# Moving the masks of one attention quad and four value products, with other PSUM banks, in a two-layer transformer block kernel

## The chip, the cores and the metric

The kernel runs on one core of one Trainium2 chip. The metric is the time of one execution on the device, in microseconds (us); the figure that counts is the median of several runs.

## The reference, cut to what matters

Input `x` has 16 batches of 256 tokens with 128 features, all float32.

```python
xn = layernorm(x)
x  = x + favor(xn) + local(xn)       # first block
xn = layernorm(x)
x  = x + attention(xn) + experts(xn) # second block

# favor (causal linear attention, 16 heads of 8, 32 random features)
phi_q, phi_k = exp(x_h @ proj.T - 0.5 * sum(x_h ** 2)) / sqrt(32)
num[t] = sum_{s <= t} (phi_q[t] . phi_k[s]) v[s];  den[t] = sum_{s <= t} phi_q[t] . phi_k[s]
favor  = layernorm(num / den @ out_w + out_b + x)

# local: 2 layers, each
h = shift_token(x); q, k, v = split(h @ wqkv)      # 8 heads of 64
q, k = rotary(l2norm(q) * q_scale), rotary(l2norm(k) * k_scale)
x = x + softmax(window(q @ k.T)) @ v @ wo          # window of 64 + 64
x = x + (a * gelu(g)) @ w2 + b2                    # a, g = layernorm(shift_token(x)) @ w1 + b1

# attention: 16 heads of 8, softmax over 256 keys
# experts: 8 experts of 256, the best two of each token weighted, and a shared one
```

## The kernel before, in words

The 16 batches are done two at a time, in 8 turns. In a turn T = 512 tokens lie on the free axis. All instructions are written out by hand, per engine, in one list each (`@block.tensor`, `@block.scalar`, `@block.vector`, `@block.gpsimd`, `@block.sync`), and ordered across engines by counting semaphores alone: `now(name, n)` is the count that a semaphore has after the n-th event of this turn.

PSUM has 8 banks. Every product that an engine will read back is a **job** `(name, k)` with a bank. The function `job` (called in the order in which PE will do the jobs) gives each a bank from a ring (`RINGS`, `RING_OF`), and notes who used the bank last and what frees it: `pe.wait_ge(*freed(name, k))` ahead of a job makes PE wait until the former user's reader is done. So the ring decides for whom a product has to wait.

A turn is, in this order: **layer 0** of the local block, **layer 1** of it, then the second block (router, experts with the attention's maxima between them, attention). The favor attention is spread through the two layers, in 8 **quads** of 4 heads (`FAVOR_AT`, `FAVOR_PV`): `favor_score` (L635, L639 on PE, into 4 banks), the causal mask as a multiply on DVE (L1472, frees each bank with `favor_p`), `favor_pv` (L652, accumulates numerator and denominator of half the batches in one bank for 4 quads), and after the fourth quad a copy to `heads` on ACT (L1220), `favor_den` (L659, spreads the denominators over rows) and on DVE `favor_out` (reciprocal L1462 and multiply L1463).

One layer, in the names of the code:

- `loc_raw` (L712): queries and keys, 8 products; DVE rotates them (L1492 to L1501, tile `lc`), ACT squares them, PE sums the squares (L698, L732).
- DVE turns the sums into roots (`rsqrt`, L1343 to L1350, and three bf16 parts up to L1517, semaphore `loc_rs`); PE transposes them (L742), ACT copies them to `lrT` (L1216), and PE spreads them over the rows: 4 products `loc_rb` (L751). DVE multiplies `lc` with them, 8 multiplies (L1525), each counted by `loc_qk`.
- **Maxima**: in two groups g = 0 and 1, PE first writes the window mask into 4 banks (L758, "claims" the banks), then adds 96 short products (L770, `loc_max`); group g reads the `lc` of the first (g = 0) or last (g = 1) four multiplies. DVE reduces the four banks (L1531, `loc_mx`) and writes negated maxima (`loc_nm`).
- PE transposes these (L782) and, for each of 4 units k, writes the scores (`loc_sT`: L794, L802, L810), ACT takes the exponentials (L1230, `loc_p`), PE sums and multiplies with the values (`loc_pv`: L822, L832), DVE divides (L1543, L1546). Values `loc_v` are products of their own (L705, and L570 for those made ahead in the turn before), copied by ACT to `lv`.
- Output product L856, then the gated unit (`glu_*`); in layer 1 the last product of the unit is L937, and DVE normalizes its result (`norm`, L1355 to L1365) for the second block, while PE does value products of the next turn (`early_value`, L570). PE then transposes (L549), ACT copies to `xn2T` (L1266), and PE does the router (L956), the queries and keys (L962), values (L966) and experts (L975, L990, L1000).
- The queries and keys are split into bf16 parts by ACT (L1279, L1304), and SP moves them by DMA (L458) into stacks that the attention's maxima (L1013) wait for.

What sets the order around the change, word for word:

```python
EARLY = 3
FAVOR_AT = {(0, "raws"): 0, (0, "sums"): 1, (0, "rb", 0): 2, (0, "rb", 2): 3,
            (0, "mean"): 4, (0, "var"): 5, (0, "gain"): 6, (1, "sums"): 7}
FAVOR_PV = {(0, "sums"): 0, (0, "rb", 0): 1, (0, "rb", 2): 2, (0, "nmT"): 3,
            (0, "var"): 4, (0, "gain"): 5, (0, "out"): 6, (1, "nmT"): 7}
```

## Time and profile before

| | |
|---|---|
| runs | 2077.65, 2084.98 and 2086.27 us, median 2084.98 |
| profiled execution | 2078.01 us, span 2076.2 us |
| busy | PE 1820.0 us (88%), DVE 1319.3 (64%), ACT 762.9 (37%), POOL 271.9 (13%) |
| granted TensorE clock | 0.949 of full speed on average |

PE is the matmul engine, PEld its weight loads, DVE VectorE, ACT ScalarE, POOL GpSimd, SP the queue that issues the DMAs. A turn takes some 256 us. Where a time is given as a point of the trace, it is in us from the start of the span; the points between 945 and 1166 belong to the end of the fourth turn's local block, its second block, and the fifth turn's two layers.

### The profile page before, as it was taken

To read this page: it belongs to the slowest core of one execution; us is meant where nothing else is said; L and a number is where in the kernel's file an instruction comes from. 1 tells how busy PE (TensorE), PEld (TensorE's weight loads), DVE (VectorE), ACT (ScalarE), POOL (GpSimd) and SP (SyncE) were. 2 spreads that over 40 slices of the span, in tenths; PEclk is the share of its full clock that TensorE was granted. 3 is DMA by queue.
4 is the path that set the end of the run, shared out by engine and by line. 5 is a ranking of instruction groups with operands and counts; after the bars stand their busy time and mean duration, and the time that the engine had idled before them with its cause. 6 is when DMAs were issued, how large, how long until landed. Compare 5 with 4: busy or idle time off the path is not lost.

```text
span 2076.2 us, 43467 instructions
## 1 busy us (share of the span) xinstructions
PE 1820.0 (88%) x18196; PEld 1068.3 (51%) x18228; DVE 1319.3 (64%) x2760; ACT 762.9 (37%) x1442; POOL 271.9 (13%) x222
## 2 busy tenths in 40 slices
PE   7888988889898898988989889898998988988988
PEld 3545545455455544555445554455544555544644
DVE  6766557665677556775567755677556775477654
ACT  3224252243433434324343244332453324533234
POOL 2010110101101111011010110111102101021010
PEclk9999999999999999999999999999999999999999
DMA  5001100011000200002000020000200002000020
GB/s 188 8 1 18 17 6 7 1 20 14 6 7 3 26 8 6 7 2 27 6 6 7 2 31 2 7 6 2 31 2 7 6 2 31 2 7 1 3 31 7
DMA packets 27764, 29.78 MB, mean 14 GB/s; under 512 B 3684, under 2 KB 26004, under 8 KB 27156
## 3 DMA queue, kind: packets, MB, share of 16 engines
q1 hardware_dynamic: 27572, 27.01, 6.8%
q8 instruction: 146, 2.39, 0.5%
q14 instruction: 46, 0.38, 0.1%
HBM read 12.06 MB, written 2.36 MB: 7 GB/s over the span
## 4 chain that ended last, share of the span: by engine, by line
PE 57%; DVE 25%; ACT 8%; issue 4%; DMA 3%; SPq 2%; ACTq 0%; DVEq 0%
PE bank L975 6%; PE bank L770 5%; PE bank L1000 5%; PE bank L990 4%; DVE ls L1543 3%; PE bank L712 3%; DMA phi<-parts 3%; DVE ftm L1462 3%; PE bank L802 3%; DVE parts L1472 2%; SPq L458 2%; ACT phi L1320 2%; DVE lc L1525 2%; PE bank L1013 2%; ACT phi L1190 2%
## 5 line engine op out<-in xcount | busy, mean ns | idle before, releaser
L1706 DVE TENSOR_REDUCE amx<-bank 128x2 f32<-128x512 f32 x256 | 161.9, 685 | 68.5 <-PE bank L1013 68.5
L1286 ACT ACTIVATE silu<-bank 128x512 f32<-128x512 f32 x144 | 84.9, 596 | 279.4 <-PE bank L975 266.8
L1694 DVE TENSOR_TENSOR mh<-bank,silu 128x512 f32<-128x512 f32 x144 | 99.6, 692 | 132.1 <-PE bank L990 129.4
L1000 PEld LDWEIGHTS bank<-w_mw,mh 128*128 128x128 f32 x1152 | 137.1, 192 | 25.4 <-issue 25.4
L975 PE MATMUL bank<-xn2T,w_mw 128*128 128x512 f32 x288 | 148.3, 634 | 0.0
L1000 PE MATMUL bank<-w_mw,mh 128*128 128x128 f32 x1152 | 143.4, 278 | 0.0
L510 POOL TENSOR_TENSOR xB<-xn2T,lsq 128x512 f32<-128x512 f32 x32 | 40.8, 1275 | 777.8 <-ACT lsq L1292 777.8
L1531 DVE TENSOR_REDUCE lmx<-bank 128x4 f32<-128x512 f32 x128 | 79.5, 684 | 98.0 <-PE bank L770 98.0
L1543 DVE RECIPROCAL ls<-bank 128x256 f32<-128x256 f32 x64 | 112.1, 1752 | 39.8 <-PE bank L822 39.6
L712 PE MATMUL bank<-hT,w_wqkv 128*128 128x512 f32 x256 | 119.1, 603 | 5.8 <-ACT hT L1260 5.7
L491 POOL TENSOR_TENSOR lc<-lc,ls 128x512 f32<-128x512 f32 x32 | 40.7, 1273 | 613.0 <-DVE lc L1501 613.0
L1726 DVE RECIPROCAL ftm<-bank 128x512 f32<-128x512 f32 x8 | 26.9, 3357 | 132.8 <-PE bank L1098 132.8
L770 PE MATMUL bank<-lc 32*64 32x128 f32 (+1 forms) x3072 | 103.3, 332 | 0.0
L770 PEld LDWEIGHTS bank<-lc 32*64 32x64 f32 (+1 forms) x3072 | 77.5, 180 | 32.9 <-issue 20.9
L802 PE MATMUL bank<-lc 32*128 32x192 f32 (+1 forms) x2048 | 88.1, 308 | 0.0
L1220 ACT ACTIVATE heads<-bank 128x512 f32<-128x512 f32 x16 | 9.6, 597 | 203.5 <-PE bank L652 203.5
L802 PEld LDWEIGHTS bank<-lc 32*128 32x128 f32 x2048 | 75.9, 185 | 14.5 <-issue 12.1
L1525 DVE TENSOR_TENSOR lc<-lc,bank 128x512 f32<-128x512 f32 x128 | 79.0, 678 | 0.2
L712 PEld LDWEIGHTS bank<-hT,w_wqkv 128*128 128x128 f32 x256 | 45.4, 190 | 63.8 <-issue 50.6
L975 PEld LDWEIGHTS bank<-xn2T,w_mw 128*128 128x128 f32 x288 | 51.1, 196 | 51.2 <-issue 50.4
L1230 ACT ACTIVATE parts<-bank 128x320 f32<-128x320 f32 x128 | 45.6, 443 | 84.1 <-PE bank L810 84.1
L758 PE MATMUL bank<-w_winmask,w_ident 128*128 128x512 bf16 x96 | 34.6, 450 | 46.3 <-DVE lc L1525 27.1
(295 smaller groups left out, 3721.1 us busy)
## 6 DMA issues: line engine op xcount, KB each, us to landing
phi<-parts SPq DMA_DIRECT2D x96, 64.0 KB
lc<-parts SPq DMA_DIRECT2D x96, 64.0 KB
w_mw<-in_mw SPq DMA_DIRECT2D x3, 1152.0 KB
x_in<-in_x SPq DMA_DIRECT2D x8, 256.0 KB, 2.8
out<-res SPq DMA_DIRECT2D x8, 256.0 KB, 2.3
w_wqkv<-in_wqkv SPq DMA_DIRECT2D x2, 768.0 KB, 7.0
w_w<-in_w SPq DMA_DIRECT2D x1, 682.0 KB, 4.1
mh<-in_rotary SPq DMA_DIRECT2D x1, 512.0 KB, 5.6
```

What stands on the lines that cost most here:

```text
L712: mm(bank_of("loc_raw", n)[:], W["wqkv"][:, l, c * P:(c + 1) * P], h, start=True, stop=True).then_inc(sem["loc_raw_ps"], 1)
L770: ins = mm(bank_of("loc_max", k + i)[u * WIN:u * WIN + m, c0:c0 + P], lc[r, c, q0 + u * WIN:q0 + u * WIN + m], lc[r, 4 + c, k0:k0 + P], st ...
L802: mm(bank_of("loc_sT", 4 * k + i)[:, c0:c0 + nq], lc[r, 4 + c, t + kt * P:t + kt * P + P], lc[r, c, t + q0:t + q0 + nq], start=False, stop ...
L975: mm(bank_of("moe_g", n)[:], W["mw3"][:, ORDER[q], i * P:(i + 1) * P], xn2T[:], start=True, stop=True).then_inc(sem["moe_g_ps"], 1)
L990: mm(bank_of("moe_u", n)[:], W["mw1"][:, ORDER[q], i * P:(i + 1) * P], xw[q % 2] if q else xn2T[:], start=True, stop=True).then_inc(sem["m ...
L1000: last = mm(bank_of("final")[:, t], mh[:, (2 * q + i) % 4, t], W["mw2"][:, ORDER[q], i, :], start=(q == 0 and j == 0 and i == 0), stop=Fal ...
L1286: A(silu[:, n % 2, :], bank_of("moe_g", n)[:], ACT.Silu).then_inc(sem["moe_silu"], 1)
L1525: V.tensor_tensor(lc[:, c, :], lc[:, c, :], bank_of("loc_rb", m)[:], ALU.mult).then_inc(sem["loc_qk"], 1)
L1531: V.tensor_reduce(lmx[:, :, i, g], bank_of("loc_max", 8 * l + h)[:].rearrange("p (j k) -> p j k", j=TT), AX.X, ALU.max).then_inc(sem["loc_ ...
L1543: V.reciprocal(lrec[:, k % 2, :], bank_of("loc_den", k)[:, 0:SEQ]).then_inc(sem["loc_rec"], 1)
L1694: V.tensor_tensor(mh[:, n % 4, :], bank_of("moe_u", n)[:], silu[:, n % 2, :], ALU.mult).then_inc(sem["moe_h"], 1)
L1706: V.tensor_reduce(amx[:, 2 * b:2 * b + 2, h], bank_of("att_max", n)[:].rearrange("p (t k) -> p t k", t=2), AX.X, ALU.max).then_inc(sem["at ...
```

## The change

It moves work and changes banks; the products themselves, their shapes and their numbers stay.

1. The score product and the masks of quad 3 leave the place between the spread roots of layer 0 and go behind unit 0 of the scores (PE) and behind the negated maxima (DVE); `favor_pv` of quad 3 goes behind unit 1.
2. Spread roots, quad 3 and the first units' sums get fixed banks (`PLACE`) instead of the ring's next one. What frees the maxima's banks changes with it.
3. The copy of favor's first half to `heads` goes behind eight exponentials, `favor_den(0)` into the gated unit of layer 0, the reciprocal (two halves now) behind the unit's gates and behind its output, the multiply into layer 1. Favor's first half keeps bank 7 until then (`favor_rec`).
4. Value product 3 of layer 0 and value product 2 of the next turn (which stood behind the router's values) join the first two: all four now follow layer 1's gated unit, with their four copies on ACT ahead of `xn2T`.

```diff
-        EARLY = 3
-        FAVOR_AT = {(0, "raws"): 0, (0, "sums"): 1, (0, "rb", 0): 2, (0, "rb", 2): 3,
+        EARLY = 4
+        FAVOR_AT = {(0, "raws"): 0, (0, "sums"): 1, (0, "rb", 0): 2, (0, "rows"): 3,
...
-        FAVOR_PV = {(0, "sums"): 0, (0, "rb", 0): 1, (0, "rb", 2): 2, (0, "nmT"): 3,
+        FAVOR_PV = {(0, "sums"): 0, (0, "rb", 0): 1, (0, "rb", 2): 2, (0, "scores"): 3,
...
+        PLACE = {("route", 0): 1, ("att_qk", 0): 0, ("att_qk", 1): 2,
+                 ("loc_rb", 1): 6, ("loc_rb", 2): 4, ("loc_rb", 3): 5, ("loc_rb", 5): 4, ("loc_rb", 6): 5, ("loc_rb", 7): 7,
+                 ("favor_score", 12): 0, ("favor_score", 13): 4, ("favor_score", 14): 5, ("favor_score", 15): 6,
+                 ("loc_nmT", 1): 6, ("loc_den", 0): 4, ("loc_pv", 0): 5, ("loc_den", 1): 6, ("loc_pv", 1): 4,
+                 ("loc_den", 2): 5, ("loc_pv", 2): 6, ("loc_den", 3): 4, ("loc_pv", 3): 5}
...
-            i = RINGS[ring][turns_of[ring] % len(RINGS[ring])]
+            i = PLACE[name, k] if (name, k) in PLACE else RINGS[ring][turns_of[ring] % len(RINGS[ring])]
...
-                    values(3)
+                    if l:
+                        values(3)
...
                         if n == 0:
-                            favor_den(l)
+                            favor_heads(l, "rows")
+                            if l:
+                                favor_den(1)
+                        if n == 1:
+                            favor_heads(l, "scores")
...
                         favor_heads(l, "var")
+                        favor_den(0)
...
                 if it + 1 < TURNS:
-                    for j in range(2):
+                    for j in range(EARLY):
                         early_value(it + 1, j)
...
-                if it + 1 < TURNS:
-                    early_value(it + 1, 2)
...
+                        if k == 4:
+                            act.wait_ge(sem["favor_pv"], now("favor_pv", 4))
...
+                        if k == 7:
+                            favor_total()
...
                     favor_heads(l, "raws")
+                    if l:
+                        favor_out(0)
...
-                    favor_out(l)
+                    favor_heads(l, "rows")
+                    if l:
+                        favor_quotient(1)
+                        favor_out(1)
...
+                        favor_quotient(0, 0)
...
+                        favor_quotient(0, 1)
```

**PE, layer 1, from the spread roots to the claims of the first maxima** (bank numbers and what each waits for; `loc_qk` counts DVE's multiplies of `lc`, `favor_p` masks of a quad). Before:

```order
L751 MATMUL bank1<-lrT,w_headrow 128x512 [waits loc_v,loc_rT]
L751 MATMUL bank2<-lrT,w_headrow 128x512 [waits favor_p]
L751 MATMUL bank3<-lrT,w_headrow 128x512 [waits favor_p]
L751 MATMUL bank4<-lrT,w_headrow 128x512 [waits favor_p]
L758 MATMUL bank2<-w_winmask,w_ident4 128x512 [waits loc_qk]
L758 MATMUL bank3<-w_winmask,w_ident4 128x512 [waits loc_qk]
L758 MATMUL bank0<-w_winmask,w_ident4 128x512 [waits loc_rT]
L758 MATMUL bank1<-w_winmask,w_ident4 128x512 [waits loc_qk]
```

Now:

```order
L759 MATMUL bank0<-lrT,w_headrow 128x512 [waits loc_v,loc_rT]
L759 MATMUL bank4<-lrT,w_headrow 128x512 [waits favor_p]
L759 MATMUL bank5<-lrT,w_headrow 128x512 [waits loc_rT]
L759 MATMUL bank7<-lrT,w_headrow 128x512 [waits loc_ss]
L766 MATMUL bank2<-w_winmask,w_ident4 128x512 [waits favor_p]
L766 MATMUL bank3<-w_winmask,w_ident4 128x512 [waits favor_p]
L766 MATMUL bank0<-w_winmask,w_ident4 128x512 [waits loc_qk]
L766 MATMUL bank1<-w_winmask,w_ident4 128x512 [waits favor_p]
```

The first claim waited for the fourth multiply, the second for the sixth; now none waits for more than the second.

**PE, layer 0, from the first half of the spread roots to the first maxima** (`phi` rows are the scores of a quad, `avz` rows its `favor_pv`). Before:

```order
L751 MATMUL bank<-lrT,w_headrow 128x512 x2
L635 MATMUL bank<-phi 128x256 x4
L639 MATMUL bank<-phi 128x128 x4
L652 MATMUL bank<-fp,avz 32x256 x4
L652 MATMUL bank<-fp,avz 32x128 x4
L751 MATMUL bank<-lrT,w_headrow 128x512
L758 MATMUL bank<-w_winmask,w_ident 128x512 x4
L770 MATMUL bank<-lc 128x128 x8
L770 MATMUL bank<-lc 64x128 x16
L770 MATMUL bank<-lc 128x128 x8
L770 MATMUL bank<-lc 64x128 x16
L652 MATMUL bank<-parts,avz 32x256 x4
```

Now:

```order
L759 MATMUL bank<-lrT,w_headrow 128x512 x2
L659 MATMUL bank<-fp,avz 32x256 x4
L659 MATMUL bank<-fp,avz 32x128 x4
L759 MATMUL bank<-lrT,w_headrow 128x512
L766 MATMUL bank<-w_winmask,w_ident 128x512 x4
L778 MATMUL bank<-lc 128x128 x8
L778 MATMUL bank<-lc 64x128 x16
L778 MATMUL bank<-lc 128x128 x8
L778 MATMUL bank<-lc 64x128 x16
```

The first maxima's third bank was freed by the eighth multiply of `lc`, its fourth by the sixth; now none of the four waits for more than the second. The second `phi` pair, quad 3, is gone from there. It stands, with its `avz` rows, around the second unit of scores instead:

```order
L790 MATMUL bank<-w_ident,lnm 128x128 x4
L802 MATMUL bank<-w_bandmask,w_ident 128x320 x4
L810 MATMUL bank<-lc 128x192 x4
L810 MATMUL bank<-lc 128x128 x4
L810 MATMUL bank<-lc 128x192 x4
L810 MATMUL bank<-lc 128x128 x4
L818 MATMUL bank<-lnmT,w_nmrow 128x192 x4
L818 MATMUL bank<-lnmT,w_nmrow 128x128 x4
L642 MATMUL bank<-phi 128x256 x4
L646 MATMUL bank<-phi 128x128 x4
L802 MATMUL bank<-w_bandmask,w_ident 128x320 x4
L810 MATMUL bank<-lc 128x192 x4
L810 MATMUL bank<-lc 128x128 x4
L810 MATMUL bank<-lc 128x192 x4
L810 MATMUL bank<-lc 128x128 x4
```

**PE, from the end of layer 1's gated unit to the experts** (`w_wqkv,hT` are value products of the next turn). Before:

```order
L937 MATMUL bank<-w_w,fqs 128x128 x8
L570 MATMUL bank<-w_wqkv,hT 128x512 x2
L549 MATMUL bank<-w_ident,ftm 128x128 x4
L956 MATMUL bank<-w_wr,xn2T 128x8 x4
L962 MATMUL bank<-xn2T,w_aw 128x512 x2
L966 MATMUL bank<-w_aw,xn2T 128x128 x4
L570 MATMUL bank<-w_wqkv,hT 128x512
```

Now:

```order
L950 MATMUL bank<-w_w,fqs 128x128 x8
L577 MATMUL bank<-w_wqkv,hT 128x512 x4
L556 MATMUL bank<-w_ident,ftm 128x128 x4
L969 MATMUL bank<-w_wr,xn2T 128x8 x4
L975 MATMUL bank<-xn2T,w_aw 128x512 x2
L979 MATMUL bank<-w_aw,xn2T 128x128 x4
```

Four value products stand ahead of the transposes, none behind.

## Rows read from the trace of the kernel before

**Rows 1.** The page's part 4: shares of the chain that ended last.

```profile
PE 57%; DVE 25%; ACT 8%; issue 4%; DMA 3%; SPq 2%; ACTq 0%; DVEq 0%
```

**Rows 2.** The waits: total us, times, longest us.

```profile
PE bank L758 <- DVE lc L1525: 27.1, 16, 2.8
```

**Rows 3.** Timeline of PE, layer 1: start, us, engine, line, op, names, form, count [idle before <-releaser].

```profile
1152.56 1.89 PE L751 MATMUL bank<-lrT,w_headrow 48*128 48x512 bf16 x4 [0.68 <-ACT lrT L1216]
1156.93 1.46 PE L758 MATMUL bank<-w_winmask,w_ident 128*128 128x512 bf16 x3 [2.49 <-DVE lc L1525]
1158.33 4.54 PE L770 MATMUL bank<-lc 32*128 32x128 f32 x96
```

**Rows 4.** Timeline of DVE, layer 1, the same stretch.

```profile
1153.20 4.87 DVE L1525 TENSOR_TENSOR lc<-lc,bank 128x512 f32<-128x512 f32 x8
1162.95 2.48 DVE L1531 TENSOR_REDUCE lmx<-bank 128x4 f32<-128x512 f32 x4 [4.88 <-PE bank L770]
```

**Rows 5.** Windows of PE: start:end, length, busy, instructions, granted clock, DMA share, GB/s.

```profile
1077.40:1084.20 6.80, 6.38 (x62) 0.50 0.01 2
1152.50:1162.70 10.20, 7.65 (x103) 0.50 0.01 2
```

**Rows 6.** Timeline of DVE, layer 0, between the roots and the maxima.

```profile
1077.82 1.95 DVE L1472 TENSOR_TENSOR fp<-bank,w_causal 128x384 f32<-128x384 f32 x4
1079.82 2.48 DVE L1525 TENSOR_TENSOR lc<-lc,bank 128x512 f32<-128x512 f32 x4
1082.22 1.94 DVE L1472 TENSOR_TENSOR parts<-bank,w_causal 128x384 f32<-128x384 f32 x4
```

**Rows 7.** Timeline of PE, layer 0, from the value product to favor's denominators.

```profile
1071.26 1.10 PE L705 MATMUL bank<-w_wqkv,hT 128*128 128x512 f32 x2
1072.29 0.71 PE L635 MATMUL bank<-phi 32*128 32x256 f32 x8
...
1085.41 0.60 PE L758 MATMUL bank<-w_winmask,w_ident 128*128 128x512 bf16 x2 [0.80 <-DVE lc L1525]
1085.95 2.63 PE L770 MATMUL bank<-lc 32*128 32x128 f32 x96
1088.51 0.86 PE L652 MATMUL bank<-parts,avz 128*32 128x256 f32 x16
...
1090.26 2.63 PE L770 MATMUL bank<-lc 32*128 32x128 f32 x96
...
1095.64 1.13 PE L659 MATMUL bank<-heads,w_den 128*128 128x512 f32 x2
```

**Rows 8.** Timeline of ACT, layer 0, the first four exponentials.

```profile
1095.73 1.43 ACT L1230 ACTIVATE fp<-bank 128x320 f32<-128x320 f32 x4 [1.88 <-PE bank L810]
```

**Rows 9.** Timeline of PE, from layer 1's unit to the router.

```profile
951.45 1.88 PE L570 MATMUL bank<-w_wqkv,hT 128*128 128x512 f32 x4
956.35 0.63 PE L549 MATMUL bank<-w_ident,ftm 128*128 128x128 f32 x4 [3.02 <-DVE ftm L1365]
957.66 1.68 PE L956 MATMUL bank<-w_wr,xn2T 128*128 128x8 f32 x8 [0.69 <-ACT xn2T L1266]
959.20 3.76 PE L962 MATMUL bank<-xn2T,w_aw 128*128 128x512 f32 x4
```

**Rows 10.** Timeline of PE, first maxima of the attention.

```profile
990.89 0.61 PE L1013 MATMUL bank<-lc,phi 48*128 48x256 bf16 x8 [3.17 <-DMA phi<-parts]
991.43 3.21 PE L975 MATMUL bank<-xn2T,w_mw 128*128 128x512 f32 x4
```

**Rows 11.** The page's part 5: group, count | busy us, mean ns | idle before.

```profile
L1543 DVE RECIPROCAL ls<-bank 128x256 f32<-128x256 f32 x64 | 112.1, 1752 | 39.8 <-PE bank L822 39.6
```

**Rows 12.** Timeline of DVE, end of layer 0 and start of layer 1.

```profile
1132.99 0.75 DVE L1640 SCALAR_TENSOR_TENSOR xB<-bank,w_cols,xB 128x512 f32<-128x512 f32 x1 [1.83 <-PE bank L926]
...
1135.62 0.69 DVE L1492 TENSOR_TENSOR lc<-bank,rot 128x512 f32<-128x512 f32 x1 [1.42 <-PE bank L712]
...
1143.45 0.69 DVE L1492 TENSOR_TENSOR lc<-bank,rot 128x512 f32<-128x512 f32 x1 [0.52 <-ACT mh L1199]
```

More of the change, by code:

```diff
@@ L275, in job @@
         def job(name, k, freed_by, count, ahead=0):
-            ring = "late" if (name, k, ahead) == ("loc_v", 2, 1) else ("quad", "wide", "quad", "wide1")[k // 4] if name == "loc_max" else "long" if (name, k) in LONG else RING_OF[name] if name in RING_OF else "short"
-            i = RINGS[ring][turns_of[ring] % len(RINGS[ring])]
+            ring = ("quad", "wide", "quad", "wide1")[k // 4] if name == "loc_max" else "long" if (name, k) in LONG else RING_OF[name] if name in RING_OF else "short"
+            i = PLACE[name, k] if (name, k) in PLACE else RINGS[ring][turns_of[ring] % len(RINGS[ring])]
             turns_of[ring] += 1
@@ L285, in favor_jobs @@
                 if quad % 4 == 0:
-                    job("favor_pv", quad // 4, "favor_att", quad // 4 + 1)
+                    job("favor_pv", quad // 4, *(("favor_att", 2) if quad else ("favor_rec", 2)))
                 for n in range(4 * quad, 4 * quad + 4):
@@ L328, in build @@
                         job("loc_sT", 4 * k + i, "loc_p", 4 * k + i + 1)
+                if n == 0:
+                    favor_jobs(l, "rows")
                 if l == 1 and n == 2:
@@ L363, in build @@
         job("att_v", 0, "att_v", 1)
-        job("loc_v", 2, "loc_v", 3, ahead=1)
         def weight_job(q):
@@ L945, in _ @@
                 if it + 1 < TURNS:
-                    for j in range(2):
+                    for j in range(EARLY):
                         early_value(it + 1, j)
@@ L1263, in _ @@
                 if it + 1 < TURNS:
-                    early_value(it + 1, 0)
+                    for j in range(EARLY):
+                        early_value(it + 1, j)
                 act.wait_ge(sem["xn2T_ps"], now("xn2T_ps", 1))
@@ L1506, in _ @@
                     favor_heads(l, "raws")
+                    if l:
+                        favor_out(0)
                     dve.wait_ge(sem["loc_sum_ps"], now("loc_sum_ps", l + 1))
```

39 lines of the change are left out of this document (24 added, 15 removed).

## The prediction

> **What bounds the kernel now.** I read the page's chain first, then the waits, then the timelines of one turn (the fifth) on PE and DVE, with the granted clock of short windows. The chain runs over PE for 57% and over DVE for 25% of the span [rows 1]: no engine bounds the whole, and in each stretch the question is who waits for whom. The waits name one place that this change touches: PE, about to claim the banks of the maxima (L758), waits for DVE's multiplies of `lc`, 16 times, 27.1 us in all, 2.8 at most [rows 2]. That is once per layer and turn.
>
> In layer 1 that wait is 2.49 us, until 1156.93 [rows 3]. DVE's eight multiplies run from 1153.20 to 1158.07, 0.61 each [rows 4]. The claims waited for the sixth (1153.20 + 6 x 0.61 = 1156.9), while the products behind them (L770, first group) need the first four alone, done by 1155.7. They start at 1158.33 and take 4.54 us, at the lower of the clock's two levels: from 1152.5 to 1162.7 the granted clock is 0.50, that is 1.2 GHz [rows 3, 5]. DVE then stands idle 4.88 us for them [rows 4].
>
> In layer 0 DVE is the bound between the roots and the maxima: masks of quad 2 (1.95), four multiplies (2.48), masks of quad 3 (1.94), and two more multiplies, without a gap [rows 6]. PE waits 0.80 at its claim and starts L770 at 1085.95, at full level here (2.63 us) [rows 7].
>
> **Layer 1: new banks for the roots.** With the claims free after the second multiply, PE makes them behind the spread roots, which end at about 1154.45 [rows 3]. The records have three of the four claims, 1158.33 - 1156.93 = 1.40 for them, 0.47 each; four take 1.9, to 1156.35, when the first four multiplies are done. L770 starts 1158.33 - 1156.35 = 2.0 us earlier. It also fills a stretch in which PE did little, so the clock should come back earlier; if L770 has a third to a half of its products at the full level, it saves a further 0.3 to 0.5 x (4.54 - 2.63) = 0.6 to 1.0. What follows (reduction on DVE, second group) is a chain behind it and moves with it. Bounds: 2.0 (no help from the clock), 3.5 (nearly all of the 1.9 as well). I take 2.8: 8 x 2.8 = **22.4 us**.
>
> **Layer 0: quad 3 moved.** Off DVE's path go 1.94 us of masks [rows 6]; off PE's go the scores (about 1.0, from L635 and L639 behind it) and the `favor_pv` between the groups (0.86) [rows 7]. Also the first group no longer waits for all multiplies. Six of them now follow quad 2 from 1079.82; two are enough to complete four. PE has `favor_pv` of quad 2, a root and four claims to do, and can start L770 at about 1082.0 instead of 1085.95, **4.0 us** earlier at the full level. The second group began 1090.26 - 1088.58 = 1.7 us behind the first [rows 7]; without `favor_pv` it is bounded by DVE's first reduction and a claim, about 1.0, so 4.7 in all.
>
> Given back: quad 3's scores now stand behind unit 0 and wait for its first exponential, since one bank is the first unit's: ACT starts at 1095.73 and does four in 1.43, so PE waits about 0.5 [rows 8]. Then 1.0 of scores, some 0.2 until DVE's first mask frees a bank, 0.8 of `favor_pv`; less the denominators' product that leaves this place, 1.0 (L659, 1.13 with overlap [rows 7]), and the wait on its quotient (0.2): 0.5 + 1.0 + 0.2 + 0.8 - 1.2 = 1.3 us. At full level layer 0 gains 4.7 - 1.3 = 3.4 us a turn.
>
> The clock speaks against that. Already now it is at 0.50 from 1077.4 to 1084.2 [rows 5], where PE had short products between gaps; the products that run there are covered by DVE. The change takes a dense value product (1.03 us [rows 7]) and a quad out of this stretch and pulls L770 towards it. If L770's first group begins at the lower level it takes up to 4.54 [rows 3] in place of 2.63 and starts at about 1084.5, since scores, `favor_pv` and claims ahead of it are slower too: it then ends at 1088.2 to 1089.0, against 1088.6 now, and with 0.7 saved at the second group the turn stands between -0.2 and +1.0. So ends: 3.4 won, 1.0 lost. Nearly every turn should see a lower-level stretch here, but in half of them it should be over when L770 starts. I take 1.7: 8 x 1.7 = **13.6 us**.
>
> The Trainium skill, TensorE: Matmul & The Clock Gate, section "What's actually happening", says that the throttled clock is the default and that activity releases it. Read strictly against this change, that rule gives layer 0 nothing, 0 in place of 13.6, and it is the first rival below.
>
> **Four value products in one place.** The two that move are 1.0 us each on PE [rows 7, 9]. Behind layer 1's unit PE now idles 3.02 us for DVE's normalization [rows 9]; two more products, about 1.8, fit, and their copies on ACT fit ahead of `xn2T`. They cost nothing. What PE saves later (1.0, and up to some 2.5 more, an estimate, if router and queries, where L962 now takes 3.76 at the lower level, run at the full one) only brings it sooner to the attention's first maxima, where it waits 3.17 us for the DMAs of the stacks [rows 10]. Those start with ACT's split of the queries and keys, which waits for DVE's router chain, which waits for the router's product: 1.54 us from L956 to L962 [rows 9], 0.7 less at the full level at best. So the gain is at most 7 x 0.7 = 4.9. The longer idle costs: L975 behind it takes 3.21 at the lower level [rows 10] where full is about 2.0; with the products around it some 1.6 a turn, in turns that escape it now. Ends: +4.9 won, 8 lost; I take **0**. If this gain is missing, it is the DMA that is late next.
>
> The value product leaves layer 0 where DVE bounds; apart from the clock that is nothing.
>
> **Favor's first half, later.** Its product (1.0) goes into a gap ahead of the unit's roots and before DVE is done with masks: nothing, or 0.1. On DVE the full reciprocal leaves layer 0's units, where DVE was not the bound. A half one takes 1.75 [rows 11]; the first fits DVE's idle 1.83 ahead of L1640 [rows 12]. The second ends about 0.3 later than the 1135.62 at which the rotations start, and a 0.52 idle at 1143.45 absorbs it [rows 12]; the multiply falls into DVE's wait for the sums. If those covers fail it costs 0.3 each: ends 0 and 5; I take **1 us**.
>
> **Sum.** -22.4 - 13.6 + 0 + 1 = -35. The profiled execution took 2078.0 (span 2076.2 and 1.8 around it): 2043. The three runs are 2077.65, 2084.98 and 2086.27, so the profiled one is with the fastest and 7 below their median; by the median it would be 2050. I predict 2045.
>
> **The rivals.** I count 0.5% (10 us) as what a measurement can tell from no change.
>
> *Layer 0 gives nothing.* L770 of layer 0 runs at the lower level in every turn. For it: rows 5 and the dense work taken out. Against: in this turn the clock was back at 1084.2 already. -22.4 + 1 + 0: 2057 to 2064. Chance 0.24.
>
> *The clock comes back early in both layers.* 8 x 3.4 and 8 x 3.3, and 4 at the router: 2078 - 57 = 2021 to 2030. For it: less idle in layer 1. Chance 0.17.
>
> *Most is given back.* Layer 1 gains only the 2.0 (16), layer 0 loses 1.0 (8), the longer DMA wait costs 5: 2078 - 3 = 2075, or 2080 by the median. For it: three clocks must go wrong together. Chance 0.09.
>
> *Slower.* The lower level holds in layer 0 from the roots through both groups and unit 0: two groups at 4.54 (+3.8), the stretch from the second group's end at 1092.89 to 1095.64 at half speed (+2.7) [rows 7], 1.3 given back, less 2.1 for earlier starts: 5.7 a turn, against 2.0 in layer 1: +3.7 x 8 = 30, 2108. It decides from the point at which the low stretch reaches the second group in most turns. Against: L770 itself is dense and in layer 1 ended such a stretch [rows 3, 5]. Chance 0.04.
>
> *The change does not do what it says* (the claims still wait for late multiplies): the instruction order with its waits shows them freed, so I give this none of its own.
>
> **Numbers.** The forecast, 2035 to 2055, has 0.46. Faster by over 0.5% hold the forecast and the first two rivals, 0.87; within 0.5%, 0.09; slower, 0.04. The range reaches over the two faster rivals: 2023 to 2066.
>
> **What would show it.** Layer 1: the claims' wait for `lc` gone from the waits (27.1 to under 5), L770 starting within 0.8 us of the fourth multiply, DVE's idle ahead of its reduction near 2 instead of 4.88. Layer 0: DVE's six multiplies in a row, first L770 some 2.5 to 4 us behind the start of the third; if it takes 4 us or more in most turns, the first rival is right. The router: PE's idle ahead of the transposes near 1.3, the wait for the stacks 5 to 6. The prediction is wrong if layer 1's L770 does not start earlier, or if quad 3's new place costs over 2 us.

## Result and profile after

| | before | after |
|---|---|---|
| runs, us | 2077.65, 2078.23, 2084.98, 2086.27 | 2051.20, 2051.39, 2054.07, 2055.52 |
| median | 2081.61 | 2052.73 |
| profiled execution (span) | 2078.01 (2076.2) | 2051.20 (2049.4) |

The ratio is 0.9862, with a 95% interval from 0.9833 to 0.9891: 1.4% faster, some 29 us. I had predicted 2045 with a range from 2023 to 2066. Between the spans of the two profiled executions the gain is 26.8 us, where the sum said 35.

The page of after, parts 1 and 4 (compare [rows 1]):

```profile
PE 1817.0 (89%) x18228; PEld 1052.5 (51%) x18228; DVE 1321.5 (64%) x2768; ACT 762.0 (37%) x1442; POOL 274.8 (13%) x222
...
PE 57%; DVE 21%; ACT 8%; SPq 6%; DMA 4%; issue 4%; ACTq 0%; DVEq 0%
```

DVE went from 25% of the chain to 21%; SP's queue and the DMAs went from 5% to 10%. The waits say the same (columns: total us, times, longest us). The wait of PE's claims for `lc`, 27.1 us in [rows 2], is no longer among them, and the wait for the stacks, 19.2 us before, heads PE's list:

```profile
PE bank L1024 <- DMA phi<-parts: 42.0, 8, 6.9
PE bank L750 <- DVE lr L1546: 36.1, 16, 2.7
PE bank L556 <- DVE ftm L1383: 13.8, 8, 4.7
```

Layer 1 of the fifth turn, timeline of PE and then of DVE, the lines that answer to [rows 3, 4] (start, us, ...):

```profile
1139.63 2.16 PE L759 MATMUL bank<-lrT,w_headrow 48*128 48x512 bf16 x4 [0.68 <-ACT lrT L1227]
1141.72 1.89 PE L766 MATMUL bank<-w_winmask,w_ident 128*128 128x512 bf16 x4
1143.54 3.72 PE L778 MATMUL bank<-lc 32*128 32x128 f32 x96
```

```profile
1140.27 4.87 DVE L1554 TENSOR_TENSOR lc<-lc,bank 128x512 f32<-128x512 f32 x8
1147.32 2.48 DVE L1560 TENSOR_REDUCE lmx<-bank 128x4 f32<-128x512 f32 x4 [2.18 <-PE bank L778]
```

The claims follow the roots without a wait. The first group starts 0.8 us behind the fourth multiply (1140.27 + 4 x 0.61 = 1142.7). DVE's idle ahead of its reduction is 2.18 instead of 4.88. The group takes 3.72 us, between the 2.63 and the 4.54 that it takes at the two levels of the clock.

Layer 0 of the same turn, DVE and PE, the lines that answer to [rows 6, 7]:

```profile
1064.66 1.95 DVE L1499 TENSOR_TENSOR fp<-bank,w_causal 128x384 f32<-128x384 f32 x4
1066.66 3.68 DVE L1554 TENSOR_TENSOR lc<-lc,bank 128x512 f32<-128x512 f32 x6
1073.55 2.48 DVE L1560 TENSOR_REDUCE lmx<-bank 128x4 f32<-128x512 f32 x4 [3.20 <-PE bank L778]
```

```profile
1066.98 1.51 PE L659 MATMUL bank<-fp,avz 128*32 128x256 f32 x16
...
1068.96 1.89 PE L766 MATMUL bank<-w_winmask,w_ident 128*128 128x512 bf16 x4
1070.78 2.71 PE L778 MATMUL bank<-lc 32*128 32x128 f32 x96
```

DVE does its six multiplies in a row and then waits 3.20 us for PE. It waited as long before (3.28), but then PE had itself waited for DVE ahead of its claims (0.80 in [rows 7]); now PE has no such wait. So PE is the bound here, and its `favor_pv` (1.51) and claims (1.89) run at the lower level, as the window says (start:end, length, PE busy, PEld busy, DVE, ACT, POOL, granted clock, DMA share, GB/s):

```profile
1066.00:1069.00 3.00, 3.00 (x24) 0.87 (x21) 2.94 (x6) 0.00 (x0) 0.00 (x0) 0.50 0.00 0
```

In four turns the first group starts 4.1 us behind the start of the third multiply, as in this one, and in the other four 2.2 us behind it.

**Where the time went.** I cut every turn at the same landmarks in each profile: the first rotation of a layer (L1492 before, L1519 after), the first and the last reduction of the layer's maxima (L1531, L1560), the first transpose behind layer 1's unit (L549, L556) and the first maxima of the attention (L1013, L1024; the last stretch goes to the next turn's rotations, in turn 8 to the end). Sums over 8 turns, us, one profiled execution each; the kernels from `banks` on are the experiments below:

| | start-up | L0 to maxima | L0 maxima | behind them | L1 to maxima | to transposes | to attention | to next turn | span |
|---|---|---|---|---|---|---|---|---|---|
| before | 25.6 | 281.9 | 55.4 | 323.8 | 218.2 | 342.0 | 326.2 | 503.1 | 2076.2 |
| after | 27.0 | 256.7 | 50.9 | 338.5 | 199.7 | 342.4 | 319.7 | 514.5 | 2049.4 |
| banks | 26.6 | 282.2 | 55.4 | 323.7 | 196.8 | 342.0 | 325.7 | 510.1 | 2062.3 |
| no_quad | 26.8 | 295.9 | 55.4 | 321.4 | 198.5 | 342.1 | 318.3 | 511.7 | 2070.0 |
| values_back | 25.9 | 248.4 | 50.9 | 338.6 | 199.1 | 342.4 | 327.5 | 513.1 | 2045.9 |
| no_quad_fill | 26.9 | 281.3 | 55.4 | 326.8 | 193.7 | 342.1 | 317.8 | 519.1 | 2063.2 |
| fill_roots | 28.4 | 250.5 | 50.9 | 338.6 | 195.5 | 343.2 | 317.5 | 513.7 | 2038.3 |
| den_in_gap | 26.3 | 259.6 | 50.9 | 329.9 | 198.2 | 342.4 | 320.1 | 513.5 | 2041.0 |
| three_early | 26.0 | 256.2 | 50.9 | 338.6 | 198.4 | 342.5 | 324.0 | 510.6 | 2047.2 |
| stack_early | 26.2 | 256.6 | 50.9 | 338.7 | 200.7 | 342.5 | 304.5 | 509.9 | 2030.1 |
| three_stack | 26.9 | 246.9 | 51.0 | 339.1 | 199.5 | 342.5 | 319.1 | 504.6 | 2029.5 |
| gate_first | 27.6 | 261.7 | 51.0 | 338.6 | 200.4 | 342.6 | 318.5 | 499.5 | 2039.9 |
| stack_den_fill | 27.1 | 251.3 | 51.0 | 330.0 | 194.5 | 342.6 | 309.2 | 503.7 | 2009.3 |
| together | 27.2 | 248.3 | 51.0 | 330.0 | 191.6 | 342.9 | 312.4 | 491.7 | 1994.9 |

So the change won 29.7 us in layer 0 up to and in its maxima, gave 14.7 back behind them, won 18.5 in layer 1 and 6.5 ahead of the attention, and shows 11.4 more behind it and 1.4 in the start-up. A caution on the column "to next turn": single turns take 61.53, 63.2, 64 or 66 us there, from turn to turn of one execution, and which turns get which differs between kernels that are the same in this part. What makes them differ is the clock. Windows of PE over this stretch in turns 1 and 2 of the kernel before, then in the same turns of the changed one (start:end, length, PE busy, granted clock, DMA share, GB/s):

```profile
220.60:283.76 63.16, 60.32 (x441) 0.97 0.01 2
477.07:538.60 61.53, 58.69 (x441) 1.00 0.01 2
```

```profile
217.54:280.75 63.21, 60.37 (x441) 0.97 0.01 2
467.72:533.68 65.96, 63.13 (x441) 0.93 0.01 2
```

In the first seven turns of every kernel whose order is the same here the stretch takes 61.5 us plus 0.47 us for each us that the clock is at its lower level in it, to within 0.2. In the kernel before that level lasts 14 us over seven turns, in the changed one 35. So a difference of 5 to 10 us in that column alone tells nothing about the work in it; it tells how long the clock was low.

### The profile page after: what moved, and what is told of

The parts are those of the page before. It is cut to its first block, busy times and chain, and to the rows that moved or that the text cites. A ratio compares the mean times of both kernels' runs of the same rounds, so it can differ in the third digit from the quotient of the medians.

```text
span 2049.4 us, 43532 instructions
## 1 busy us (share of the span) xinstructions
PE 1817.0 (89%) x18228; PEld 1052.5 (51%) x18228; DVE 1321.5 (64%) x2768; ACT 762.0 (37%) x1442; POOL 274.8 (13%) x222
## 4 chain that ended last, share of the span: by engine, by line
PE 57%; DVE 21%; ACT 8%; SPq 6%; DMA 4%; issue 4%; ACTq 0%; DVEq 0%
SPq L465 6%; PE bank L778 5%; PE bank L986 4%; PE bank L1011 4%; PE bank L1001 4%; DMA phi<-parts 4%; PE bank L719 3%; PE bank L810 3%; DVE ls L1575 3%; PE bank L868 2%; PE bank L1024 2%; ACT phi L1338 2%; PE bank L659 2%; ACT phi L1201 2%; ACT lc L1338 2%
## 5 line engine op out<-in xcount | busy, mean ns | idle before, releaser
L986 PE MATMUL bank<-xn2T,w_mw 128*128 128x512 f32 x288 | 154.9, 659 | 0.0
L1560 DVE TENSOR_REDUCE lmx<-bank 128x4 f32<-128x512 f32 x128 | 79.5, 684 | 60.9 <-PE bank L778 60.9
L1760 DVE RECIPROCAL ftm<-bank 128x512 f32<-128x512 f32 x8 | 26.9, 3358 | 132.5 <-PE bank L1109 132.5
L778 PE MATMUL bank<-lc 32*64 32x128 f32 (+1 forms) x3072 | 94.8, 309 | 0.0
L778 PEld LDWEIGHTS bank<-lc 32*64 32x64 f32 (+1 forms) x3072 | 71.7, 166 | 30.8 <-issue 12.5
L1024 PE MATMUL bank<-lc,phi 48*128 48x256 bf16 x512 | 49.7, 292 | 42.0 <-DMA phi<-parts 42.0
L1242 ACT ACTIVATE lnmT<-bank 128x512 bf16<-128x512 bf16 x32 | 19.2, 598 | 153.6 <-PE bank L790 153.6
```

The lines of the kernel that those rows point to most:

```text
L778: ins = mm(bank_of("loc_max", k + i)[u * WIN:u * WIN + m, c0:c0 + P], lc[r, c, q0 + u * WIN:q0 + u * WIN + m], lc[r, 4 + c, k0:k0 + P], st ...
L986: mm(bank_of("moe_g", n)[:], W["mw3"][:, ORDER[q], i * P:(i + 1) * P], xn2T[:], start=True, stop=True).then_inc(sem["moe_g_ps"], 1)
L1024: ins = mm(o[:, qt * SEQ:(qt + 1) * SEQ], qst[r, hh, t + qt * P:t + qt * P + P], kst[r, hh, t:t + SEQ], start=True, stop=True)
```

## Experiments

Every kernel was timed several times (4 to 6 executions) beside the kernel before, whose median lay between 2079.8 and 2083.4. Times below are medians, with the ratio to before and its 95% interval. Landmarks come from one profiled execution of each, which is not always a typical one.

**1. Layer 1's banks alone (banks).** The kernel before and

```diff
+        PLACE = {("loc_rb", 5): 4, ("loc_rb", 6): 5, ("loc_rb", 7): 7}
```

> The kernel before with one thing of the change: the last three spread roots of layer 1 get banks 4, 5 and 7, so that the claims of the maxima's first group wait for the second multiply alone. Theory A (the gains add up by stage, as the two traces' landmarks say): layer 1 gives 2.3 us a turn, 18.5 in all, 2078 to 2060, and nothing else moves. Theory B (the clock couples the stages; the on-record 22.4 was right for layer 1 alone and part of it was given back elsewhere by the rest of the change): 2056 or less. Against both: under 10 us gained, if the low clock at the first group eats it. The claims' wait for lc should fall from 27.1 us to under 14 (layer 0's eight waits stay) in either case.

2068.3 us, ratio 0.9936 [0.9917, 0.9956], 13 us faster by the ratio. Layer 1 up to its maxima gave 218.23 - 196.75 = 21.5 us, 2.7 a turn, and nothing else moved except the column "to next turn", where 7.0 were lost. So the stage gave more than Theory A's 18.5, the whole less than either theory said. Three entries of a table bring 13 of the change's 29 us, and the on-record 2.8 a turn was near.

**2. The change without quad 3 (no_quad).** Banks and all four value products, quad 3 and favor's first half as before.

> The changed kernel without the move of quad 3 and favor's first half: the kernel before with layer 1's banks and with all four value products behind layer 1's unit. Theory A: moving the values costs 4.9 us by the landmarks (6.5 won before the attention's maxima, 11.4 lost behind them, because the maxima wait for the same DMAs with a longer idle), so 5 us above the kernel with the banks alone, about 2065. Theory B (values cost nothing, the on-record 0, and what is lost behind the maxima comes from starting earlier in another phase): equal to the kernel with the banks alone within 2 us, about 2060. In both, layer 0 up to its maxima stays at 35.2 us a turn; if it shortens here by a microsecond a turn, part of layer 0's gain belongs to the value product that left it, not to quad 3.

2070.2 us, ratio 0.9937 [0.9916, 0.9958]: no difference from the banks alone, as Theory B had it for the whole. But inside, two large terms cancel. Ahead of the attention it won 7.4, and **layer 0 lost 13.7**, though one product fewer stands there; both theories had left layer 0 as it was. Timeline of PE of this kernel, layer 0, fifth turn:

```profile
1076.71 0.39 PE L753 MATMUL bank<-lrT,w_headrow 48*128 48x512 bf16 x1
1080.41 0.82 PE L760 MATMUL bank<-w_winmask,w_ident 128*128 128x512 bf16 x3 [3.31 <-DVE lc L1522]
1081.16 4.10 PE L772 MATMUL bank<-lc 32*128 32x128 f32 x95
```

PE idles 3.31 us for DVE's multiplies and then runs the first group at the lower level, 4.10 instead of 2.63. In all eight turns that group took 3.65 us or more; in the kernel before, in three.

**3. Idle work in the product's stead (no_quad_fill).** The kernel of experiment 2, and in layer 0 two products that nobody reads, in PE's waits for the roots and for the last multiplies:

```diff
                     pe.wait_ge(*freed("loc_rT", l))
+                    for _ in range((1, 0)[l]):
+                        mm(bank_of("loc_rT", l)[:], W["wqkv"][:, l, 0:P], W["wqkv"][:, l, 0:T], start=True, stop=True)
...
                             pe.wait_ge(*freed("loc_max", k + i))
+                            if k + i == 0:
+                                mm(bank_of("loc_max", 0)[:], W["wqkv"][:, l, 0:P], W["wqkv"][:, l, 0:T], start=True, stop=True)
```

(The bank's real writer overwrites each of them; both stand in layer 0 alone.)

> The kernel with layer 1's banks and the four moved values, quad 3 in its old place (layer 0 up to its maxima: 295.9 us in 8 turns, against 282.2 with the value product still in layer 0; its first maxima group takes 4.1 us at the lower clock), with two idle products of 128x512 in layer 0, one in PE's wait for the roots and one in its wait for the last multiplies ahead of the claims. They stand in for the value product that left and do nothing else. Theory A (taking dense work out of this stretch costs it the clock, and that is the 14 us): layer 0 up to its maxima back at 275 to 284 us, the first group mostly near 2.6, 12 to 18 us faster, 2052 to 2058. Theory B (the 14 us come from the other ring positions and waits that the moved product left): layer 0 stays near 296 or grows, 2070 or more.

2059.2 us, ratio 0.9893 [0.9868, 0.9918], 11 us faster than without them, just under the 12 to 18 of Theory A. Layer 0 went from 295.9 to 281.3 us, and its first group took 2.63 us in all eight turns:

```profile
1075.32 1.12 PE L763 MATMUL bank<-w_wqkv 128*128 128x512 f32 x2 [2.12 <-DVE parts L1473]
1076.29 1.05 PE L764 MATMUL bank<-w_winmask,w_ident 128*128 128x512 bf16 x4
1077.27 2.63 PE L776 MATMUL bank<-lc 32*128 32x128 f32 x96
```

The granted clock over that group, without the two products and with them (windows of all engines as above):

```profile
1081.10:1085.30 4.20, 4.20 (x101) 3.19 (x104) 0.00 (x0) 0.00 (x0) 0.00 (x0) 0.59 0.01 4
```

```profile
1077.27:1079.90 2.63, 2.63 (x101) 2.05 (x104) 0.00 (x0) 0.00 (x0) 0.00 (x0) 1.00 0.03 6
```

Work that computes nothing makes the kernel faster, and nothing else was changed. That the 14 us of experiment 2 are the clock is shown. The rest of the turn is not untouched: layer 1, where no product was added, gave 4.8 us, and the column "to next turn" took 7.4 more. The Trainium skill, TensorE: Matmul & The Clock Gate, section "What's actually happening", says that the throttled state is the default and that activity releases it; this pair of kernels agrees with it (0.59 over the group without the two products, 1.00 with them).

**4. Values put back in the changed kernel (values_back).** The edit of part 4 of the change undone, with the banks that belong to it, all else kept.

> The changed kernel with the four value products put back as in the kernel before (one in layer 0, one behind the router's values), all else kept. Theory A: 5 us faster than the changed kernel, some 2046, with PE's wait for the stacks back near 3 us a turn and layer 0 as short as in the changed kernel. Theory B (layer 0's gain needs the product gone, or the values are worth nothing): 2051 to 2056. A value product back in layer 0, where DVE was the bound before, costs at most 1.0 us a turn if PE is the bound there now: then layer 0 up to the maxima grows from 32.1 to 33.1 a turn and the whole is 2051 to 2054, though the router's part gains its 5.

2048.2 us, ratio 0.9843 [0.9823, 0.9863], against 0.9862 for the changed kernel; the intervals overlap, so the whole is not told apart. By the landmarks layer 0 won 8.4 us although a 1 us product came back into each turn, and the first group took 2.63 in all eight. Neither theory had said so; one had feared 1 us a turn more. Ahead of the attention 7.8 were lost. Windows of PE, layer 0 up to its maxima, the third and the fourth turn of the changed kernel and then of this one:

```profile
533.68:567.57 33.89, 28.97 (x283) 0.85 0.03 9
789.28:820.47 31.19, 25.97 (x283) 0.95 0.03 9
```

```profile
529.77:560.97 31.20, 26.86 (x283) 0.95 0.03 9
786.37:816.85 30.48, 25.40 (x283) 1.00 0.03 10
```

Here too the length goes with the clock: 30.5 us where it is at full level throughout (four turns of this kernel, none of the changed one), 31.2, 32.7 and 33.9 where the window shows 0.95, 0.90 and 0.85.

**5. Three of the four early (three_early).** The last product back in layer 0, the other three behind layer 1's unit.

(One bank of the router and one of the queries are others as well.)

> The changed kernel with the last value product of layer 0 back in layer 0, and the other three still behind layer 1's unit. So far: with that product in layer 0 the stretch from the rotations to the maxima took 248.4 us over 8 turns, without it 256.7, although the product itself is 1 us of work. Theory A (it is the dense product that keeps PE at the full clock through the roots, and the router's 8 us come from the value product that left the router): layer 0 at 248 to 250, transposes to maxima at 319 to 321, so 7 to 8 us faster than the changed kernel, some 2044 to 2046. Theory B (the router's 8 us need all four products in the gap): transposes to maxima back near 326, 2050.

2040.2 us, ratio 0.9808 [0.9776, 0.984]; its runs lie between 2032 and 2053. Layer 0 came out at 256.2, not at 249: four turns took 32.7 to 34.1 us, the other four 30.5 to 31.2. Theory A is half right there: a dense product in this place makes the full level more frequent, not certain. Ahead of the attention Theory B was right: 324.0. What the fourth product does is seen in the group of the queries and keys, from the groups by line (count, busy us, mean ns of one, idle) of the kernel before, of this one and of the changed one:

```profile
L962 PE MATMUL bank<-xn2T,w_aw 128*128 128x512 f32 x32 | 30.1, 1096 | 0.0
```

```profile
L973 PE MATMUL bank<-xn2T,w_aw 128*128 128x512 f32 x32 | 29.2, 1067 | 0.0
```

```profile
L975 PE MATMUL bank<-xn2T,w_aw 128*128 128x512 f32 x32 | 17.5, 673 | 0.0
```

With four products in the gap the changed kernel runs them at the full level in seven of eight turns (the last turn has none); with two or three almost no turn does. But four are no guarantee: in `den_in_gap`, `fill_roots` and `together` three, three and none of the turns have them at full level.

**6. Denominators in an earlier gap (den_in_gap).**

```diff
                         mm(o[:], W["center"][:], h, start=True, stop=True).then_inc(sem["glu_mean_ps"], 1)
+                        favor_den(0)
...
                         favor_heads(l, "var")
-                        favor_den(0)
```

> The changed kernel with the product of favor's denominators of the first half moved from behind the variances (where the roots of the gated unit now find PE busy with it) to the gap of 0.78 us ahead of the variances. Theory A (that product costs layer 0's gated unit what the trace shows: 25.98 from the output product to the next rotations against 25.03 before): 0.6 to 0.9 us a turn back, 5 to 7 us, some 2045 to 2047. Theory B (the loss is quad 4's scores and masks, or the low clock there whatever stands in it): under 2 us.

2033.1 us (2026 to 2044), ratio 0.9781 [0.975, 0.9812]. The stretch behind layer 0's maxima fell from 338.5 to 329.9: 8.6 us, 1.07 a turn. Timeline of PE of the changed kernel, then of this one:

```profile
1104.81 0.98 PE L642 MATMUL bank<-phi 32*128 32x256 f32 x8 [0.46 <-DVE fp L1499]
...
1107.59 1.58 PE L666 MATMUL bank<-heads,w_den 128*128 128x512 f32 x2
1109.01 1.05 PE L891 MATMUL bank<-w_ident,rs 128*128 128x128 f32 x8
```

```profile
1100.75 1.02 PE L666 MATMUL bank<-heads,w_den 128*128 128x512 f32 x2
...
1103.18 0.71 PE L642 MATMUL bank<-phi 32*128 32x256 f32 x8 [0.46 <-DVE fp L1499]
...
1105.45 1.13 PE L891 MATMUL bank<-w_ident,rs 128*128 128x128 f32 x8 [0.55 <-DVE rs L1368]
```

In the changed kernel the product stood where the unit's roots were already there, at the lower level (1.58), and L891 came behind it. In the gap ahead of the variances it delays nothing that matters, and the products behind it run at full level too (L642 in 0.71 instead of 0.98). The median moved more than this stretch does, 17 us by the two ratios. The profiled execution is one of the slow ones of this kernel: three took 2038 to 2044 us at a granted clock of 0.955 to 0.957, three 2026 to 2028 at 0.961 or 0.962.

**7. Idle work ahead of the root transposes (fill_roots).** The first half of the edit of experiment 3 in the changed kernel, one product in layer 0 and two in layer 1.

> The changed kernel with idle work added: while PE waits for the roots it does one product of 128x512 in layer 0 and two in layer 1, into the bank that the root transposes overwrite; nobody reads them. Theory A (the clock of the first maxima group is set by how busy PE was ahead of it): layer 0 up to its maxima falls from 32.1 to about 31.1 a turn as it does with the value product, and layer 1 from 25.0 to about 24 (the first group 2.63 instead of 3.7), together 12 to 16 us faster, 2036 to 2040, though 24 us of PE work were added. Theory B (what counts is not the clock but which banks and products stand in the stretch): 0 to 4 us slower, since a product of 1.0 delays the transposes where the wait was 1.81 or shorter.

2036.4 us, ratio 0.9791 [0.9767, 0.9814]. Layer 0 gave 6.2 us, its first group at 2.63 in all eight turns; layer 1 gave 4.2, since its first group escaped the lower level in only two turns. Theory A holds, its size for layer 1 does not (8 us were expected there).

**8. The stacks sooner (stack_early).** ACT's first split no longer waits for DVE's router chain:

```diff
-                act.wait_ge(sem["route_d"], now("route_d", 1))
-                A(rsm[:, 4:6, :], rsm[:, 2:4, :], ACT.Exp).then_inc(sem["route_exp"], 1)
                 act.wait_ge(sem["att_qk"], now("att_qk", 2))
                 act.wait_ge(sem["stack_in"], prior("stack_in"))
                 A(parts[:, :, 0, :], aqk, ACT.Copy).then_inc(sem["att_part1"], 1)
+                act.wait_ge(sem["route_d"], now("route_d", 1))
+                A(rsm[:, 4:6, :], rsm[:, 2:4, :], ACT.Exp).then_inc(sem["route_exp"], 1)
```

> The changed kernel with ACT's first split of queries and keys ahead of the router's exponential instead of behind it: ACT then does not wait for DVE's router chain, and SP can issue the first stack DMA about 1.8 us sooner (the split starts near 949.4 in place of 951.3). Theory A (the stacks' transfers are one unbroken train of 24 that sets the start of the attention's maxima): PE's wait for them falls by 1.8 us in each of 8 turns, from 42 to some 28 in all, and the time by 12 to 15, to 2037 to 2039. Theory B (the train's end is set elsewhere, by the later parts or by the queue's own rate): the last landing does not move, the time stays within 3 us of the changed kernel. Theory C: the gain at the maxima is given back since the clock there is low anyway or DVE's router weights come 1 us later: 4 to 8 us.

2026.7 us, ratio 0.9736 [0.9714, 0.9758], 55 us below before by the ratio. The split starts 13.1 us behind the first transpose instead of 14.9, and the stretch to the attention's maxima became 15.2 us shorter, 1.9 a turn: Theory A. Timeline of the changed kernel, ACT's split, the first and last DMAs of SP, and the wait:

```profile
951.26 1.04 ACT L1299 ACTIVATE parts<-fqs 128x1024 bf16<-128x1024 f32 x1
```

```profile
952.32 1.34 SPq L465 DMA_DIRECT2D phi<-parts  x2
...
967.32 1.27 SPq L465 DMA_DIRECT2D phi<-parts  x2
```

```profile
976.75 1.03 PE L1024 MATMUL bank<-lc,phi 48*128 48x256 bf16 x8 [5.10 <-DMA phi<-parts]
977.71 3.78 PE L986 MATMUL bank<-xn2T,w_mw 128*128 128x512 f32 x4
```

The same of this kernel, ACT and PE:

```profile
944.54 1.06 ACT L1297 ACTIVATE parts<-fqs 128x1024 bf16<-128x1024 f32 x1
```

```profile
970.22 0.61 PE L1024 MATMUL bank<-lc,phi 48*128 48x256 bf16 x8 [3.44 <-DMA phi<-parts]
```

From the split's end to the first maxima it is 22.6 to 26.3 us, by turn, in before and after alike, and 21.3 to 26.4 in the other kernels. In every turn of every kernel the first of the train's 24 DMAs is issued 0.02 or 0.03 us behind the split's end and the last 15.2 to 16.5 us behind it; no edit here shortened the train by more than that scatter. The median moved by more than the 19 us between the profiles, but the profiled execution is the slowest of the four (2031.9 us at a granted clock of 0.958; the fastest took 2022.7 at 0.964).

**9. Both (three_stack).** Experiments 5 and 8 together.

> The value product of layer 0 back as above, three products behind layer 1's unit, and the early split for the stacks. The early split alone gave 26 us on top of the changed kernel by the medians (12 to 15 were expected), 15 of them between the transposes and the maxima, which is 1.9 a turn. If the parts add up (A): 8 more from layer 0: 2018 to 2020. If layer 0's gain is lost since the turns start in another phase of the clock (B): 2024 to 2027.

2037.1 us, ratio 0.9789 [0.9767, 0.9812]: slower than the early split with four products. The expected sum failed, and so did its rival, whose reason was layer 0. Layer 0 was short (246.9), but the stretch to the attention took 319.1 against 304.5: with three products the queries run at the lower level, ACT gets them late, and the split starts 15.7 us or more behind the first transpose in the seven full turns. Ahead of an early split the fourth product is worth 14.7 us, without one 4.3; there ACT waits for the router's chain ahead of the split.

**10. Needed work into the wait (gate_first).** The gate products of the fourth expert move ahead of the first maxima:

```diff
-                    if q > 2:
+                    if q == 3 or q > 4:
                         expert_gate(q)
...
                     att_maxes(q, 1)
                     expert_out(q - 1)
+                    if q == 3:
+                        expert_gate(4)
                     att_maxes(q, 2)
```

> The changed kernel with the two gate products of the fourth expert ahead of the first attention maxima instead of between the first and the second pair. PE then does 1.9 us of needed work inside its wait for the stacks (42.0 us in 8 turns, 6.9 at most). Theory A (the stacks' landing alone sets the first maxima, and PE is the bound behind them): the wait falls by some 1.9 a turn to about 27, the maxima start where they did (319 to 321 from the transposes in 8 turns), and the part behind them shortens by 1.9 us a turn or, at the lower clock, up to 3.8 where the gate product now runs right behind the wait: 15 to 30 us, 2022 to 2036. Theory B (behind the first maxima DVE's reductions are the bound, and PE's order there is worth nothing): within 3 us of the changed kernel.

2029.1 us, ratio 0.9728 [0.9691, 0.9766], with runs from 2013 to 2042. The wait fell as expected, from 42.0 us to 27.1, and the stretch behind it by 15.0 us. Its shortest turn is 59.67 us, in this kernel and in `together`; in all twelve others it is 61.5 or more. Theory A; PE is the bound behind the landing. Between the two profiles the whole is only 9.5 us shorter, since layer 0 took 5.0 us more in this one.

```profile
PE bank L1026 <- DMA phi<-parts: 27.1, 8, 5.0
```

**11 and 12. Combined.** Experiments 6, 7 and 8 in one kernel (stack_den_fill), and then 10 as well (together).

> The changed kernel with three of the edits tried alone: the early split for the stacks, the product of favor's denominators ahead of the variances, and the idle products ahead of the root transposes (one in layer 0, two in layer 1). By the profiles' landmarks these gave 15 us (transposes to maxima), 8.5 us (behind layer 0's maxima) and 9 us (the two root stretches, 1.4 of start-up taken off). If they add up: 2051 less 33, 2014 to 2020. If the clock's phase takes a part: 2022 or more.

> The same three edits and the gate products ahead of the first maxima. PE's wait for the stacks is about 3 us a turn with the early split, so the 1.9 us of gate products still fit: 10 to 15 us below the kernel without them, 2003 to 2010. If the wait is used up in most turns, the product pushes the first maxima and only 5 us are left: 2013.

2011.8 us, ratio 0.9666 [0.9642, 0.9691], and **1993.6 us, ratio 0.9581 [0.9557, 0.9605]**, 87 us below before and about 59 below the changed kernel. Both are better than expected. Not every part adds up: the stretch ahead of the attention takes 309.2 and 312.4 us, against 304.5 with the early split alone, and where the queries ran slower than at the full level in five of the seven full turns and in all seven. The page and the waits of the last:

```profile
PE 1811.5 (91%) x18276; PEld 1054.3 (53%) x18276; DVE 1317.4 (66%) x2768; ACT 762.5 (38%) x1442; POOL 275.0 (14%) x222
...
PE 59%; DVE 21%; ACT 8%; issue 4%; SPq 4%; DMA 3%; ACTq 0%; DVEq 0%
```

```profile
PE bank L1028 <- DMA phi<-parts: 9.5, 6, 3.3
```

It issues 48 matmuls more than the changed kernel and PE is busy 5.5 us less, at a granted clock of 0.972 of full speed instead of 0.954.

## Why the prediction was right or wrong

The whole fell 8 us short of the sum (26.8 for 35), well inside the range. By the landmarks: layer 1 gave 4 less than forecast, layer 0 with favor's first half 2 more, the stretch ahead of the attention 6.5 where 0 was taken, and the one behind its first maxima took 11.4 where 0 was taken; start-up and transposes took 2.

- **Layer 1, 22.4 us: right in kind, 4 us too high.** Alone, the banks give 21.5 up to the maxima; in the changed kernel 18.5. The signs named for it are there: the wait is gone, the group starts 0.7 to 0.9 us behind the fourth multiply, DVE's idle is 1.9 to 2.6 us, and the group takes 3.5 to 4.1 us, so part of it has the full level. With the banks alone it starts 0.5 us behind the fourth multiply; why later here stays open.
- **Layer 0, 13.6 us: right in kind, and near in sum with some luck.** Up to and in the maxima it is 29.7 us, 3.7 a turn, where I had taken about 3.0 (the 1.7 and the 1.3 given back). `values_back` and `banks` differ by quad 3 and favor's first half: 38.2 us, 4.8 a turn, against the 4.7 of the prediction at full level. So the clock took some 1.0 a turn and not 1.7. The start of the first group that I had at full level, 1082.0, is 2.2 us behind the third multiply, and four turns have it; in the other four it is 4.1, and the first group took at most 3.34 us where I feared 4.54. From the last reduction to the output product it is 16.6 against 15.0 us, 1.6 a turn given back, for which I had 1.3. That leaves 29.7 - 12.5 = 17.2 us. It is one execution, and the clock in it could have fallen otherwise.
- **Favor's first half, 1 us: wrong.** The failing step is "its product (1.0) goes into a gap ahead of the unit's roots ...: nothing, or 0.1". I had looked at an idle of PE in the old order, which quad 4 and the lower clock fill in the new one. Against a place where it is covered it costs 1.07 a turn, 8.6 us (experiment 6). Against the kernel before, the stretch from the output product to the next rotations grew by 0.8 to 1.0 us in five turns and became 1.2 shorter in two, 2.2 us longer in sum over eight. The two halves of the reciprocal cost nothing that shows.
- **The four value products, 0: three real terms, taken as one zero.** That the extra products fit the idle ahead of the transposes was right (3.02 became 1.30), and so was the wait for the stacks (5.25 on average, 5 to 6 said). Ahead of the attention 6.5 to 8 us were won, over my bound of 4.9: the split starts 0.8 us earlier, where I had at most 0.7. In layer 0 the phrase "apart from the clock that is nothing" leaves out what mattered: by the profiles the clock there is 8.4 us in the changed kernel (experiment 4; with the product back, experiment 5 shows 0.6 and experiment 9 against 8 shows 9.8) and 14 without quad 3. I had charged it to layer 0 alone.
- **The longer idle, at most 8 lost, taken at 0 by setting it against the gain: the step behind most of the miss.** Behind the attention's first maxima 11.4 us more were spent. In the kernel before, three turns had waited 1.3 us or less for the stacks and then ran at full level throughout (61.53 us); in the changed one these turns wait 3.2 to 6.4 us and take 63.2 to 66.0, which is 8.1 of the 11.4, as the term on record had it ("some 1.6 a turn, in turns that escape it now"). That it is the clock is shown by the windows. That the longer wait brought it is argued: over all kernels the turns without a low clock there had waited 0 to 2.9 us and those with one 1.2 to 6.9, but `banks` and `values_back`, whose waits are near those of before (21.3 and 22.6 us in all, for 19.2), spent 7 and 10 us more as well.
- **Layer 0's move and the values are coupled.** With the value product gone and quad 3 in place the layer is 1.7 us a turn longer than with the banks alone; with quad 3 moved as well it is 1.0 longer than with the value product back. The prediction summed the parts as if each stood alone.
- **Rivals.** "Layer 0 gives nothing" fell: its mark, 4 us or more from the third multiply in most turns, was met in four of eight, and even those started earlier than before (6.1 us or more). "The clock comes back early in both" fell in layer 1 (3.5 to 4.1 us for the group) and in layer 0, where every turn still shows a low stretch ahead of the maxima. "Most is given back" and "Slower" fell with the time itself.
- **The number.** 2045 was forecast and 2052.7 measured. The two terms that were furthest off, +6.5 and -11.4, have opposite signs, and that is luck.

## What to carry to other kernels

- Before moving dense work out of a stretch where another engine is the bound, look at the clock of what PE does next there: the product that looks free under its cover may be what keeps PE fast. Test it by putting products that nobody reads in its place.
- When a bank table makes a claim wait for late readers, changing three entries can be worth as much as reordering a stage; try it alone first.
- When a wait for DMAs grows, ask what starts their train and what needed work fits into the wait. Here those two edits gave 26 and 28 us by the ratios, each about as much as the whole change.

## What I had not expected of the hardware

- Two dense products that nobody reads moved the next 96 products from 3.65 to 4.58 us down to 2.63, in all eight turns at once (experiments 2 and 3).
- The same stretch of one execution takes 31.2, 32.7 or 33.9 us (changed kernel, layer 0 up to the maxima, by turn) with the same instructions, at a granted clock of 0.95, 0.90 and 0.85. Whole runs of one kernel differ likewise: in experiment 10 the slowest took 2041.7 us at 0.953 and the fastest 2013.4 at 0.962. So small edits need both several runs and the landmarks of a profile, read with the clock beside them.
